# Attention over four images: inverse sums applied to the mixed banks, a sixth transferred group, half of the transferred tiles in heads and tails

## The chip, the core and the metric

The kernel runs on one core of one Trainium2 chip. A core has TensorE (matrix products, transposes), VectorE, ScalarE, Pool (GpSimd) and SyncE, each with a queue of instructions that it works off in order; they wait for one another on semaphores. TensorE writes PSUM; VectorE and ScalarE read it; Pool sees only SBUF. Transfers are issued by SyncE here and run on 16 DMA engines. The metric is the time of one execution in microseconds (us); shown are medians of several runs.

## The reference, cut to what matters

For each of four images x of 128 channels by 1024 positions:

```
y   = group_norm(x, 4 groups) * gamma + beta
q, k, v = (w_qkv y + b_qkv) split in three        # 128 channels each
w   = softmax(q^T k / sqrt(128))                  # 1024 x 1024
out = x + w_out (v w^T) + b_out
```

All in float32.

## The kernel before, in words

Weights are folded first: the scores become z^T y plus a bias per key, with z a projection of y, and v already contains w_out. Nothing is left behind the mix but a bias and the sum with x.

The queries of the four images make 32 blocks of 128, eight for an image; four blocks make a group (0 to 7). The loop has a turn for each block. Each engine's queue has its own copy of this loop, with the order written out by hand; what is said below of a turn holds for the engine named.

- TensorE (from L645): the scores of the block two turns ahead (`block_scores`, L700): three fp32r products, z and y each parted in a head (rounded to fp32r) and a tail (the rest), over two halves of 512 keys, 6 instructions. Then `turn` (L720), eight transposes, for blocks of groups 0, 6 and 7. Then pieces of the next image's projections (`projection`, L665): Z0 and Z1 in turns 4 and 7 of an image, the value jobs V0, V1, V2 in turns 5, 6 and the next image's 0. Then some tiles of an earlier group's mix (`mix`, L737), as the table `MIX` says; a group has 8 tiles of 128 keys by 512 queries. The mix of group g begins in turn 4g + 7.
- VectorE: `maximum` of the block two turns ahead (L513), with the key bias; for a turned block, half of the copy out of PSUM (L534); for a block of groups 1 to 5 `flip` (L547), a transposition of 32x32 squares into a staging buffer; pieces of the projections (`z_tail` L487, `projection_vectors`); `results` of a group (L556); `inverse_sum` of the block two turns ahead (L530); statistics of the image two ahead.
- ScalarE: copies out of PSUM, `exponentials` (L359) with the row sums, `y_head`.
- Pool: `normalise` (L293) multiplies each block's probabilities by its inverse sums; `normalised_input`, `y_tail`, and `z_tail` (L281) of the second half.
- SyncE: `swap` (L228) of a group: 16 transfers of 128 KB from staging to home, which put the flipped squares in their places; `store` of results.

What a block goes through: scores, maximum, exponential, inverse sum, normalisation on Pool, then either transposes on TensorE or flip and transfer, then the mix. Groups 1 to 5 are mixed as whole f32 tiles (`L765`), groups 6 and 7 as three fp32r products of heads and tails (`L760` to `L762`). `probs` has four buffers; a block's exponential waits until the block four before it has been turned or flipped.

An image's first scores wait for its z tail:

```
                if b > 0 and i == 0:
                    pe.wait_ge(s_z_lo, HALVES * (b - 1) + 1)
                    pe.wait_ge(s_y_lo, HALVES * b)
```

Of the kernel before, what the change touches and what calls it, by code (L numbers as in the profile page):

```python
# [5 lines left out]
def attention_kernel(nc, x, vectors, weights, out):  # L6
# [38 lines left out]
    SWAPPED = range(1, 6)  # L45
    SPLIT_GROUPS = (6, 7)
    HOME = (0, 1, 0, 1, 0, 1)
    SWAP = 16 * SQ * SQ
    MIX = {4: [(0, 1)], 5: [(0, 1)], 6: [(0, 1)], 7: [(0, 1)], 8: [(0, 1)], 9: [(0, 1)], 10: [(0, 2)],
           27: [(5, 2)], 28: [(5, 3)], 29: [(5, 2)], 30: [(5, 1), (6, 3)], 31: [(6, 5)]}  # L50
# [8 lines left out]
    with ctx:  # L59
# [19 lines left out]
        minus_mean = sb("minus_mean", [128, 128])  # L79
# [19 lines left out]

        y = sb("y", [C, 2, N])  # L100
        y_hi, y_lo = sb("y_hi", [C, 2, N], fp32r), sb("y_lo", [C, 2, N], fp32r)
        z_hi, z_lo = sb("z_hi", [C, 2, N], fp32r), sb("z_lo", [C, 2, N], fp32r)
        z_full = sb("z_full", [C, HALF])
        v = sb("v", [128, 2, KT, C])
        v_hi, v_lo = sb("v_hi", [128, KT, C], fp32r), sb("v_lo", [128, KT, C], fp32r)

        key_bias = sb("key_bias", [128, 2, BLOCKS])
        neg_max = sb("neg_max", [128, BLOCKS])
        first_max = sb("first_max", [128, 1])
        row_sum = sb("row_sum", [128, BLOCKS])  # L110
        inv_sum = sb("inv_sum", [128, BLOCKS])
        probs = sb("probs", [128, RING, N])

        with nc.sbuf_tensor("crossed", [128, 4, GROUP], fp32) as crossed:
            pass
        pt_hi_7 = sb("last_turned_head", [128, KT, HALF], fp32r)
        sb("home_of_group_5", [128, KT, HALF], fp32r)
        pt_hi_6 = sb("group_6_turned_head", [128, KT, HALF], fp32r)
        pt_lo_7 = sb("last_turned_tail", [128, KT, HALF], fp32r)
        pt_lo_6 = sb("group_6_turned_tail", [128, KT, HALF], fp32r)  # L120
        PT_HI, PT_LO = {6: pt_hi_6, 7: pt_hi_7}, {6: pt_lo_6, 7: pt_lo_7}
        result = sb("result", [C, 2, HALF])

# [4 lines left out]
        DEV, MINUS_MEAN, VARIANCE = 400, 408, 416  # L128
# [34 lines left out]
        s_v_lo = sem("last_v_tail_ready")  # L163
        s_y = sem("y_ready")
# [11 lines left out]
        s_inv = sem("inv_sum_ready")  # L176
# [5 lines left out]
        s_swapped = [sem("squares_swapped_even"), sem("squares_swapped_odd")]  # L182
        s_mixed = sem("mixed_tiles_done")
        s_result = sem("result_ready")
        s_stored = [sem("stored_even"), sem("stored_odd")]
# [21 lines left out]

        def copy_of_turned(home, n, j):

            return home[:, 4 * j:4 * j + 4, n % QB * 128:(n % QB + 1) * 128]  # L210

        def whole_home(group):
            return crossed[:, HOME[group], :].rearrange("p (v q) -> p v q", v=KT)

# [4 lines left out]
        def _(sp):  # L219
# [7 lines left out]

            def swap(group):  # L228
                sp.wait_ge(s_flipped, QB * group)
                if group > 1:  # L230
                    sp.wait_ge(s_mixed, KT * (group - 1))
                for k in range(SQ):
                    for g in (0, 2, 1, 3):
                        t = g ^ k
                        sp.dma_start(crossed[32 * t:32 * t + 32, group % 2, g * N:(g + 1) * N],  # L235
                                     crossed[32 * g:32 * g + 32, 2 + group % 2, t * N:(t + 1) * N]
                                     ).then_inc(s_swapped[group % 2], 16)
# [6 lines left out]
            swap(1)  # L244
            for group in range(2, 6):
                swap(group)
                store(group - 2)
            for group in range(4, GROUPS_OF_FOUR):
                store(group)
            for g in range(HALVES):  # L250
                sp.wait_ge(s_stored[g], 16 * BATCHES)

        @block_ctx.gpsimd
        def _(pool):
# [12 lines left out]
            pool.tensor_scalar(minus_mean[:, :], group_mean[:, :], -1.0, None, ALU.mult).then_inc(s_const, 1)  # L267
# [13 lines left out]
            def z_tail(b):  # L281
                pool.wait_ge(s_z_full, b)
                pool.tensor_tensor(z_lo[:, b % 2, HALF:N], z_full[:, :], z_hi[:, b % 2, HALF:N].bitcast(fp32),
                                   ALU.subtract).then_inc(s_z_lo, 1)

# [7 lines left out]
            def normalise(b, i):  # L293
                pool.wait_ge(s_inv, BLOCKS * b + i + 1)
                pool.tensor_scalar(probs[:, i % RING, :], probs[:, i % RING, :], inv_sum[:, i:i + 1], 1.0,  # L295
                                   ALU.mult, ALU.mult).then_inc(s_probs, 1)
# [12 lines left out]
            normalise(0, 0)  # L309
            rstd_of(1, 2, 2)  # L310
            normalise(0, 1)
            for b in range(BATCHES):
                for i in range(BLOCKS):
                    behind = 0 < b < BATCHES - 1 and i == 3
                    if behind:
                        y_tail(b + 1, 0)
                    if b == 0 and i in (2, 3):
                        y_tail(1, i - 2)
                    if after(b, i, 2)[0] < BATCHES:
                        normalise(*after(b, i, 2))  # L320
                    if behind:
                        y_tail(b + 1, 1)
                    if 0 < b < BATCHES - 1 and i == 0:
                        rstd_of(b + 1, b + 2, b + 2)
                    if i == (0 if b == 0 else 1) and b + 1 < BATCHES:
                        normalised_input(b + 1)
                    if i == 7 and b + 1 < BATCHES:
                        z_tail(b + 1)

        @block_ctx.scalar  # L330
        def _(act):
# [7 lines left out]
            def value_copy(b, job, bank):  # L339
                lo, hi = V_TILES[job]  # L340
                if b == 2:
                    act.wait_ge(s_mixed, KT * (HALVES * (b - 1) - 1) + hi)
                act.activation(v_hi[:, lo:hi, :] if b == BATCHES - 1 else v[:, b % 2, lo:hi, :],
# [3 lines left out]
            def projection_copy(b, job, bank):  # L347
# [4 lines left out]
                half = slice(0, HALF) if job == Z0 else slice(HALF, N)  # L352
                act.activation(z_hi[:, b % 2, half], bank, ACT.Identity, bias=z_bias[:, :]).then_inc(s_z_hi, 1)  # L353
                if job == Z1:
                    if b >= 2:
                        act.wait_ge(s_z_lo, HALVES * (b - 1))
                    act.activation(z_full[:, :], bank, ACT.Identity, bias=z_bias[:, :]).then_inc(s_z_full, 1)

            def exponentials(b, i):  # L359
                act.wait_ge(s_max, BLOCKS * b + i + 1)  # L360
                freed = BLOCKS * b + i - RING
# [4 lines left out]
                act.activation(probs[:, i % RING, :], scores[:, i % 2, :], ACT.Exp,  # L366
                               bias=neg_max[:, i:i + 1], scale=-1.0, accum_out=row_sum[:, i:i + 1]).then_inc(s_exp, 1)

            def turned_copy(n):
                group = n // QB  # L370
                if group == 6:
                    act.wait_ge(s_swapped[0], swaps(4))
                if group == 7:
                    act.wait_ge(s_mixed, KT * 5)
                act.wait_ge(s_turned, 2 * turns(n) + 1)
                if group not in SPLIT_GROUPS:
                    act.activation(copy_of_turned(whole_home(group), n, 0), turned_tiles(0), ACT.Copy).then_inc(s_copied[0], 1)
                    return
                for j in range(2):
# [506 lines left out]
```

## Time and profile before

| | |
|---|---|
| time, median of 3 runs | 146.07 us (144.9 to 148.31) |
| span of the profiled execution | 143.7 us; its own time beside the span is not listed, the median lies 2.4 us above it |
| TensorE busy | 133.6 us (93%), 589 matmuls |
| VectorE, ScalarE, Pool busy | 103.9, 67.7, 57.1 us |
| granted TensorE clock | 0.997 mean |
| transfers of groups 1 to 5 | 80 of 128 KB, 2.3 us to landing |
| chain that ended last | PE 66%, DVE 14%, SP's queue 7% |

In the profile PE is TensorE, PEld its weight loads, DVE VectorE, ACT ScalarE, POOL Pool, SPq the queue of SyncE. L12 is line 12 of the kernel. A tile's name stands left of the arrow where it is written. Successive matmuls overlap, so the time of one is longer than the distance to the next; prices are taken from start to start. The chain of waits is followed back from the last instruction, at each step to what released it.

### The profile page before, as it was taken

Reading aid. Unit: us, or ns where it says so; the run is one execution under the profiler, and the core shown is the slowest. Engines: PE = TensorE matmul, PEld = TensorE weight load, DVE = VectorE, ACT = ScalarE, POOL = GpSimd, SP = SyncE. Lnnn points to the kernel's source line nnn. Section 1 sums busy time; section 2 is a strip of 40 time slices with the busy share of each in tenths; the row PEclk is TensorE's granted clock in tenths of the full one; section 3 lists DMA queues with packets and bytes.
Section 4 is the critical chain, followed back from the end, with each engine's and each line's share of the span. In section 5 each row is a group of like instructions: output and inputs, shape, how many; then the busy total and the mean of one; then the engine's idle time right before and its main releaser. Section 6 shows DMA issues by size and latency. Waiting matters only on the chain.

```text
span 143.7 us, 1862 instructions
## 1 busy us (share of the span) xinstructions
PE 133.6 (93%) x589; PEld 94.4 (66%) x589; DVE 103.9 (72%) x201; ACT 67.7 (47%) x122; POOL 57.1 (40%) x66
## 2 busy tenths in 40 slices
PE   7999999997499979997999999999999999999990
PEld 7978579873367635665655556766776666768770
DVE  0597587799978999899496987898763787463402
ACT  3164858763266526543361364455843666353000
POOL 6032347963334666633355556433543213330000
PEclk9999999999999999999999999999999999999998
DMA  4940000000045976983598539973996001000211
GB/s 159 310 188 0 0 5 0 0 2 0 0 101 117 206 165 141 206 200 109 109 203 197 152 66 206 206 182 81 212 203 168 0 0 73 0 0 0 80 70 73
DMA packets 6154, 15.07 MB, mean 105 GB/s; under 512 B 1664, under 2 KB 1664, under 8 KB 6144
## 3 DMA queue, kind: packets, MB, share of 16 engines
q1 hardware_dynamic: 5856, 14.69, 41.3%
q10 hardware_dynamic: 288, 0.27, 0.5%
q8 instruction: 5, 0.08, 0.3%
q14 instruction: 5, 0.04, 0.1%
HBM read 2.36 MB, written 2.10 MB: 31 GB/s over the span
## 4 chain that ended last, share of the span: by engine, by line
PE 66%; DVE 14%; SPq 7%; issue 5%; ACT 4%; DMA 2%; DVEq 0%
PE mixed L765 22%; SPq L235 7%; PE scores L715 5%; PE scores L714 5%; PE turned L731 5%; PE scores L717 5%; DVE scores L527 5%; PE scores L773 4%; DVE crossed L552 4%; ACT probs L366 3%; PE mixed L760 3%; PE mixed L762 3%; PE mixed L761 3%; PE turned L661 2%; PE mixed L661 2%
## 5 line engine op out<-in xcount | busy, mean ns | idle before, releaser
L295 POOL TENSOR_SCALAR probs<-probs,inv_sum 128x1024 f32<-128x1024 f32 x32 | 35.9, 1122 | 63.7 <-DVE inv_sum L532 63.7
L527 DVE TENSOR_SCALAR_CACHE_REDUCE scores<-scores,key_bias 128x1024 f32<-128x1024 f32 x31 | 40.0, 1289 | 13.9 <-PE scores L717 13.8
L366 ACT ACTIVATE probs<-scores,neg_max 128x1024 f32<-128x1024 f32 x32 | 35.7, 1115 | 18.7 <-DVE scores L527 17.7
L765 PE MATMUL mixed<-crossed,v 128*128 128x512 f32 x80 | 37.7, 593 | 1.0 <-DMA crossed<-crossed 1.0
L714 PE MATMUL scores<-y_hi,z_hi 128*128 128x512 f32 x62 | 34.6, 558 | 0.3 <-DVE z_lo L489 0.3
L552 DVE STREAM_TRANSPOSE crossed<-probs 128x1024 f32<-128x1024 f32 x20 | 24.8, 1241 | 0.0
L715 PE MATMUL scores<-y_lo,z_hi 128*128 128x512 f32 x62 | 24.4, 394 | 0.0
L765 PEld LDWEIGHTS mixed<-crossed,v 128*128 128x128 f32 x80 | 14.1, 190 | 11.6 <-issue 11.0
L717 PE MATMUL scores<-y_hi,z_lo 128*128 128x512 f32 x62 | 19.3, 392 | 0.0
L714 PEld LDWEIGHTS scores<-y_hi,z_hi 128*128 128x128 f32 x62 | 11.7, 189 | 8.8 <-issue 5.7
L715 PEld LDWEIGHTS scores<-y_lo,z_hi 128*128 128x128 f32 x62 | 11.7, 189 | 7.0 <-issue 5.5
L717 PEld LDWEIGHTS scores<-y_hi,z_lo 128*128 128x128 f32 x62 | 11.6, 188 | 2.8
L731 PEld LDWEIGHTS turned<-ident,probs 128*128 128x128 f32 x96 | 11.1, 141 | 2.4 <-issue 1.0
L731 PE MATMUL turned<-ident,probs 128*128 128x128 f32 x96 | 12.5, 273 | 0.1
L532 DVE RECIPROCAL inv_sum<-row_sum 128x1 f32<-128x1 f32 x32 | 5.0, 157 | 7.4 <-ACT probs L366 6.6
L561 DVE SCALAR_TENSOR_TENSOR result<-mixed,out_bias,xs 128x512 f32<-128x512 f32 x8 | 5.9, 733 | 6.1 <-PE mixed L762 6.1
L353 ACT ACTIVATE z_hi<-turned,z_bias 128x512 fp32r<-128x512 f32 x6 | 4.1, 686 | 9.1 <-PE turned L695 9.1
L767 PE MATMUL mixed<-crossed,v 128*128 128x512 f32 x16 | 8.0, 592 | 0.0
L381 ACT ACTIVATE last_turned_head<-turned 128x512 fp32r<-128x512 f32 x8 | 4.3, 595 | 7.6 <-PE turned L731 7.6
L278 POOL TENSOR_TENSOR y_lo<-y,y_hi 128x512 fp32r<-128x512 f32 x6 | 7.7, 1280 | 0.0
L544 DVE TENSOR_TENSOR last_turned_tail<-turned,last_turned_head 128x512 fp32r<-128x512 f32 x8 | 5.1, 684 | 3.5 <-ACT last_turned_head L381 3.5
L381 ACT ACTIVATE group_turned_head<-turned 128x512 fp32r<-128x512 f32 x8 | 4.3, 594 | 6.9 <-PE turned L731 6.9
(147 smaller groups left out, 168.9 us busy)
## 6 DMA issues: line engine op xcount, KB each, us to landing
crossed<-crossed SPq DMA_DIRECT2D x80, 128.0 KB, 2.3
out_dram<-result SPq DMA_DIRECT2D x8, 256.0 KB, 2.5
xs<-in_x_dram SPq DMA_DIRECT2D x2, 512.0 KB, 6.4
xs<-in_x_dram SPq DMA_DIRECT2D x3, 256.0 KB, 5.0
xs<-in_x_dram ACTq DMA_DIRECT2D x1, 256.0 KB, 3.5
ws<-in_weights_dram SPq DMA_DIRECT2D x1, 256.0 KB, 3.7
vecs<-in_vectors_dram ACTq DMA_DIRECT2D x1, 3.0 KB, 3.9
```

The source lines that it names most:

```text
L235: sp.dma_start(crossed[32 * t:32 * t + 32, group % 2, g * N:(g + 1) * N], crossed[32 * g:32 * g + 32, 2 + group % 2, t * N:(t + 1) * N]).t ...
L295: pool.tensor_scalar(probs[:, i % RING, :], probs[:, i % RING, :], inv_sum[:, i:i + 1], 1.0, ALU.mult, ALU.mult).then_inc(s_probs, 1)
L366: act.activation(probs[:, i % RING, :], scores[:, i % 2, :], ACT.Exp, bias=neg_max[:, i:i + 1], scale=-1.0, accum_out=row_sum[:, i:i + 1]) ...
L381: act.activation(copy_of_turned(PT_HI[group], n, j), turned_tiles(j), ACT.Copy).then_inc(s_turned_hi, 1)
L527: dve.tensor_scalar(scores[:, i % 2, :], scores[:, i % 2, :], key_bias[:, b % 2, i:i + 1], None, ALU.subtract, ALU.min, accum_out=neg_max[ ...
L552: dve.transpose(crossed[:, 2 + group % 2, :].rearrange("p (tv u c) -> p tv u c", u=QB, c=32)[:, :, u, :], probs[:, n % RING, :].rearrange( ...
L714: pe.matmul(to[h], z_hi[:, b % 2, query], y_hi[:, b % 2, halves[h]], start=True, stop=False)
L715: pe.matmul(to[h], z_hi[:, b % 2, query], y_lo[:, b % 2, halves[h]], start=False, stop=False)
L717: mm = pe.matmul(to[h], z_lo[:, b % 2, query], y_hi[:, b % 2, halves[h]], start=False, stop=True)
L731: mm = pe.transpose(turned[:, j, k * 128:(k + 1) * 128], probs[:, n % RING, key:key + 128], ident[:, :])
L765: mm = pe.matmul(bank, v[:, b % 2, k, :], at, start=first, stop=final)
L767: mm = pe.matmul(bank, v[:, b % 2, k, :], whole_home(group)[:, k, :], start=first, stop=final)
```

## The change

- The probabilities of groups 0 to 6 are no longer normalised block by block. Pool's `normalise` and VectorE's `inverse_sum` stay for the last group (blocks 28 to 31) alone. For the other groups VectorE makes one reciprocal of four columns (`group_inverse_sums`); SyncE stores it into a scratch in DRAM, element by element (`inv_out`), in front of the group's `swap`, and behind it loads it back, spread over all 128 partitions (`inv_in`). VectorE multiplies the mixed bank by it (`scaled`, in the place of `results`), and Pool adds x (`residual`). `out_bias` is added to x by ScalarE (`add_out_bias`).
- `flip` and the turns of group 0 wait for the exponential.
- Group 6 is flipped and transferred too, not turned. Its mix stands at the end, between two halves of 256 queries of group 7 (`mix_last`).
- Of groups 1 to 5 the tiles 4 to 7 (pairs 2 and 3), of group 6 all, are parted in heads (ScalarE, `swapped_heads`, 128x1024 for a pair of tiles) and tails (Pool, `tails`; for group 6 VectorE, `last_tails`), and mixed as three fp32r products. The values are parted for this by Pool (`part_values`).
- The first z tail of an image goes from VectorE to Pool, reading a copy that ScalarE makes; the channel statistics move from turns 4 and 5 to 2 and 3; the mean is negated on VectorE instead of by a second matmul.

The core of the diff:

```diff
-    SWAPPED = range(1, 6)
-    SPLIT_GROUPS = (6, 7)
+    SWAPPED = range(1, 7)
+    LAST = GROUPS_OF_FOUR - 1
+    PARTED = {group: (2, 3) for group in range(1, 6)} | {6: (0, 1, 2, 3)}
+    WHOLE = 4
     MIX = {4: [(0, 1)], 5: [(0, 1)], 6: [(0, 1)], 7: [(0, 1)], 8: [(0, 1)], 9: [(0, 1)], 10: [(0, 2)],
-           27: [(5, 2)], 28: [(5, 3)], 29: [(5, 2)], 30: [(5, 1), (6, 3)], 31: [(6, 5)]}
+           27: [(5, 2)], 28: [(5, 2)], 29: [(5, 2)], 30: [(5, 2)]}
...
+            def inv_out(group):
+                sp.wait_ge(s_inv, group + 1)
+                sp.dma_start(inv_scratch[group, :].rearrange("(u p) -> p u", u=QB),
+                             inv_sum[:, QB * group:QB * group + QB],
+                             allow_slow_non_contiguous=True).then_inc(s_scratch, 16)
+
+            def inv_in(group):
+                sp.wait_ge(s_scratch, 16 * (group + 1))
+                if group >= 2:
+                    sp.wait_ge(s_scaled, group - 1)
+                sp.dma_start(inv_rows[:, group % 2, :],
+                             inv_scratch[group:group + 1, :].to_broadcast([128, HALF])).then_inc(s_inv_rows[group % 2], 16)
...
+            inv_out(0)
+            inv_in(0)
+            for group in SWAPPED:
+                inv_out(group)
                 swap(group)
+                inv_in(group)
+                if group >= 2:
+                    store(group - 2)
...
+            def z_tail(b, h):
+                half = slice(h * HALF, (h + 1) * HALF)
+                pool.wait_ge(s_z_full, HALVES * (b - 1) + h + 1)
+                pool.tensor_tensor(z_lo[:, b % 2, half], z_full[:, h, :], z_hi[:, b % 2, half].bitcast(fp32),
                                    ALU.subtract).then_inc(s_z_lo, 1)
...
+            def tails(group, pair):
+                pool.wait_ge(s_head, parts(group, pair))
+                pool.tensor_tensor(home_pair(group, pair), home_pair(group, pair).bitcast(fp32),
+                                   head_pair(group, pair).bitcast(fp32), ALU.subtract).then_inc(s_tail, 1)
...
+                    if QB * LAST <= n + 2 < BATCHES * BLOCKS:
+                        normalise(n + 2)
...
+                    if i == 0 and b > 0:
+                        tails(2 * b - 2, 3) if b > 1 else None
+                        residual(2 * b - 3) if b > 1 else None
+                    if i == (1 if b == 0 else 2) and not last:
                         y_tail(b + 1, 0)
...
+                    if i == 2 and not last:
+                        part_values(b)
+                    if i == 3 and b > 0:
+                        tails(2 * b - 1, 2)
+                    if i == 4 and b > 0:
+                        if not last:
+                            y_tail(b + 1, 1)
+                        tails(2 * b - 1, 3)
+                        residual(2 * b - 2)
+                    if i == 4 and not last:
+                        z_tail(b + 1, 0)
+                    if i == 7 and not last:
+                        z_tail(b + 1, 1)
+                    if i == 7 and 0 < b and not last:
+                        tails(2 * b, 2)
+            residual(5)
+            residual(6)
...
+            # ScalarE, in a turn, behind exponentials and y_head
+                    if 11 <= n < 28 and i in (3, 7):
+                        swapped_heads(n // QB - 1, 2)
+                    if n >= 12 and i in (4, 0) and n <= 28:
+                        swapped_heads(n // QB - 2, 3)
...
+            # ScalarE, at the head of a turn
+                    if n >= 30:
+                        swapped_heads(6, 2 * (n - 30))
+                    if not swapped(n):
+                        turned_copy(n)
+                    if n >= 30:
+                        swapped_heads(6, 2 * (n - 30) + 1)
...
+            # VectorE, behind the loop
+            last_tails(0)
+            turned_tails(30)
+            scaled(5)
+            last_tails(1)
+            turned_tails(31)
+            last_tails(2)
+            last_tails(3)
+            last_result(0, mixed[:, 1, 0:256])
+            scaled(6)
+            last_result(1, scores[:, 0, 0:256])
...
+            # TensorE, behind the loop
-            mix(GROUPS_OF_FOUR - 1, KT)
+            mix_last(0, mixed[:, 1, 0:256])
+            mix(6, KT)
+            mix_last(1, scores[:, 0, 0:256])
```

## Rows read from the trace of the kernel before

**Rows 1.** Windows: stretch, length, busy of PE, PEld, DVE, ACT, POOL; clock, DMA share, GB/s.
```profile
29.27:40.24 10.97, 8.10 (x37) 5.39 (x37) 10.86 (x21) 4.98 (x10) 4.10 (x4) 1.00 0.00 0
40.24:53.85 13.61, 12.57 (x49) 8.43 (x49) 11.86 (x23) 6.85 (x12) 7.44 (x7) 1.00 0.71 156
53.85:63.20 9.35, 9.35 (x34) 5.84 (x34) 8.45 (x16) 4.79 (x9) 5.83 (x5) 1.00 0.82 180
63.20:87.14 23.94, 22.61 (x83) 14.04 (x82) 19.78 (x39) 11.13 (x19) 10.91 (x10) 1.00 0.61 144
87.14:93.85 6.71, 6.71 (x29) 4.63 (x28) 5.26 (x11) 2.54 (x7) 3.47 (x3) 1.00 0.95 211
93.85:109.82 15.97, 15.97 (x70) 10.88 (x70) 12.55 (x26) 9.88 (x18) 6.15 (x6) 1.00 0.75 175
109.82:140.46 30.64, 30.60 (x140) 21.92 (x139) 15.18 (x28) 10.89 (x20) 5.20 (x5) 1.00 0.09 31
```

**Rows 2.** Chain that ended last: start, us on the chain, what, instructions.
```profile
40.24 0.58 SPq L235
...
51.42 2.29 DMA crossed<-crossed
53.85 2.81 PE mixed L765 x6
...
77.50 2.58 PE mixed L765 x6
...
81.00 0.46 PE scores L717 x2
...
95.23 0.67 PE turned L661 x6
...
106.37 0.87 PE turned L731 x8
```

**Rows 3.** Groups by form: busy us, mean ns of one, idle before, releaser.
```profile
L527 DVE TENSOR_SCALAR_CACHE_REDUCE scores<-scores,key_bias 128x1024 f32<-128x1024 f32 x31 | 40.0, 1289 | 13.9 <-PE scores L717 13.8
L366 ACT ACTIVATE probs<-scores,neg_max 128x1024 f32<-128x1024 f32 x32 | 35.7, 1115 | 18.7 <-DVE scores L527 17.7 <-DVE neg_max L522 0.7
L552 DVE STREAM_TRANSPOSE crossed<-probs 128x1024 f32<-128x1024 f32 x20 | 24.8, 1241 | 0.0
L278 POOL TENSOR_TENSOR y_lo<-y,y_hi 128x512 fp32r<-128x512 f32 x6 | 7.7, 1280 | 0.0
L544 DVE TENSOR_TENSOR last_turned_tail<-turned,last_turned_head 128x512 fp32r<-128x512 f32 x8 | 5.1, 684 | 3.5 <-ACT last_turned_head L381 3.5
L532 DVE RECIPROCAL inv_sum<-row_sum 128x1 f32<-128x1 f32 x32 | 5.0, 157 | 7.4 <-ACT probs L366 6.6
L353 ACT ACTIVATE z_hi<-turned,z_bias 128x512 fp32r<-128x512 f32 x6 | 4.1, 686 | 9.1 <-PE turned L695 9.1
L290 POOL TENSOR_SCALAR y<-xs,norm_a,norm_b 128x1024 f32<-128x1024 f32 x3 | 3.6, 1192 | 0.2
L337 ACT ACTIVATE y_hi<-y 128x1024 fp32r<-128x1024 f32 x3 | 3.2, 1052 | 0.0
L489 DVE SCALAR_TENSOR_TENSOR z_lo<-turned,z_bias,z_hi 128x512 fp32r<-128x512 f32 x3 | 2.1, 708 | 0.0
L307 POOL TENSOR_TENSOR y_lo<-y,y_hi 128x384 fp32r<-128x384 f32 x1 | 1.0, 1017 | 1.7 <-ACT y_hi L399 1.7
```

**Rows 4.** Timeline of SyncE's queue, the fifth transfer's sixteen issues: start, us, what.
```profile
98.10 10.03 SPq L235 DMA_DIRECT2D crossed<-crossed  x16
```

**Rows 5.** DMA queues (packets, MB, share of 16 engines' span) and issues (KB, us to landing).
```profile
q1 hardware_dynamic: 5856, 14.69, 41.3%
q10 hardware_dynamic: 288, 0.27, 0.5%
...
crossed<-crossed SPq DMA_DIRECT2D x80, 128.0 KB, 2.3
```

**Rows 6.** Waits of TensorE: us in total, times, longest us.
```profile
PE turned L648 <- DVE mean_var L452: 3.6, 2, 2.6
```

More of the change, by code:

```diff
@@ L112, in attention_kernel @@
+        inv_sum = sb("inv_sum", [128, BATCHES * BLOCKS])
         probs = sb("probs", [128, RING, N])
[L114 to L120 removed]
@@ L206, in swaps, with parts, head_slot, home_pair @@
             return SWAP * len([g for g in SWAPPED if g <= group and g % 2 == group % 2])
+        def parts(group, pair):
+            return sum(len(PARTED[g]) for g in range(1, group)) + PARTED[group].index(pair) + 1
+        def head_slot(group, pair):
+            return pair if group == 6 else 2 * (group % 2) + pair - 2
+        def home_pair(group, pair):
+            return HOME[group % 2][:, :].rearrange("p (g w) -> p g w", g=SQ)[:, :, 256 * pair:256 * pair + 256]
+        def head_pair(group, pair):
+            return heads[:, head_slot(group, pair), :].rearrange("p (g w) -> p g w", g=SQ)
+        def tile_of(home, k, tiles):
+            return home.rearrange("p (g v u c) -> p v u g c", g=SQ, v=tiles, u=QB)[:, k, :, :, :]
         def copy_of_turned(home, n, j):
             return home[:, 4 * j:4 * j + 4, n % QB * 128:(n % QB + 1) * 128]
-        def whole_home(group):
-            return crossed[:, HOME[group], :].rearrange("p (v q) -> p v q", v=KT)
         def turned_tiles(j):
@@ L375, in turned_copy @@
[L375 to L379, printed above, removed]
-                    act.wait_ge(s_turned, 2 * turns(n) + j + 1)
-                    act.activation(copy_of_turned(PT_HI[group], n, j), turned_tiles(j),
-                                   ACT.Copy).then_inc(s_turned_hi, 1)
+                if n // QB == LAST:
+                    act.wait_ge(s_swapped[1], swaps(5))
+                    for j in range(2):
+                        act.wait_ge(s_turned, 2 * turns(n) + j + 1)
+                        act.activation(copy_of_turned(pt_hi, n, j), turned_tiles(j), ACT.Copy).then_inc(s_turned_hi, 1)
+                    return
@@ L735, in _, with three_products @@
             tiles_mixed = [0] * GROUPS_OF_FOUR
+            def three_products(bank, value, head, tail, first, final):
+                value_hi, value_lo = value
+                pe.matmul(bank, value_hi, head, start=first, stop=False)
+                pe.matmul(bank, value_hi, tail, start=False, stop=False)
+                return pe.matmul(bank, value_lo, head, start=False, stop=final)
             def mix(group, count):
@@ L750, in mix @@
                         pe.wait_ge(s_v, 3 * (b + 1))
[L751 removed]
+                        if b == BATCHES - 1:
                             pe.wait_ge(s_v_lo, 3)
[L753 to L757 removed]
```

375 lines of the change are left out of this document (224 added, 151 removed).

## Prediction, before any run of the changed kernel

> **What bounds the kernel now.** Blocks are numbered 0 to 31 through the four images; turn n of the loop issues the scores of block n+2. I cut the span at the events that the change touches and read the busy times by stage [rows 1]. From 29.27 to 40.24 us VectorE is the bound: 10.86 of 10.97 us busy, TensorE 8.10. From 40.24 to 53.85 the first transfer is: the chain of waits [rows 2] goes through its sixteen issues to the landing at 51.42 + 2.29, and TensorE starts the first transferred tile at 53.85. From there on TensorE is busy for 9.35 of 9.35, 22.61 of 23.94, 6.71 of 6.71, 15.97 of 15.97 and 30.60 of 30.64. So up to 53.85 a gain must come from VectorE or the transfer, after that from TensorE, as long as nothing new stops TensorE. The granted clock is 1.00 (2.4 GHz) in all these stages.
>
> **TensorE's prices** [rows 2], start to start: a whole f32 tile is two instructions, 2 x 2.58/6 = 0.86; an fp32r product is 0.46/2 = 0.23, so a parted tile is 0.70; eight transposes 0.87; scores 6 x 0.23 = 1.40; three value tiles 0.67. The change parts 20 tiles of groups 1 to 5, 20 x 0.16 = 3.3 us, and drops the transposes of group 6, 4 x 0.87 = 3.5 us: all on the path this would be minus 6.8. No row shows an fp32r product over the 32-element chunks that a parted tile streams; its price lies between 0.23 and the 0.43 of an f32 instruction. I take 0.23, since whole tiles stream such chunks already.
>
> **Up to the first tile (minus 1.7).** VectorE loses a reciprocal per block with its wait for the exponential (32 x 157 ns, 7.4 us of idle before them) and the z tail of 708 ns [rows 3]; the flip waits for the exponential, no longer for Pool. It gains a negated mean (0.2) and a reciprocal per group; two statistics move two turns ahead, into turns 2 and 3. I walk its queue with 1.20 from a maximum to the next operation, 1.15 for a flip, 0.6 for a copy or a half's statistics, 0.2 for a key bias, and TensorE's scores where they are later: the maxima of blocks 2 to 8 start at 18.05, 20.85, 23.55, 26.1, 29.9, 32.25 and 34.8, the flip of block 7 runs from 36.0 to 37.15. With the group's reciprocal SyncE could start at 37.3, 2.9 ahead of 40.24 [rows 2]. But in front of the sixteen transfers now stands the store of the inverse sums, 512 single elements. Its issue I take at 0.6, as a transfer's (10.03/16) [rows 4]; its packets lie between nothing and 32 per DMA engine at 162 ns, the mean of queue q1 (41.3% of 16 x 143.7 over 5856), 5.2 us; short ones are nearest to q10's mean, 40 ns (0.5%, 288), so 1.3 [rows 5], half of it hidden under the issues: 0.6. The Trainium skill (DMA: Bandwidth & Descriptors, Rules for kernel authors) says that a non-contiguous last dimension lowers to one descriptor per element, which speaks against this store; no row shows such a transfer. First tile: 53.85 - 2.9 + 1.2 = 52.15. TensorE is there at about 48.5 (turns 4 to 10 by the prices, 20.6, and scores, from 26.5) and waits some 3.5.
>
> **The new wait (plus 4.0 and plus 3.8).** The first z tail of the next image leaves VectorE for Pool, into turn 4 of an image, and stands there behind the last pair's tail of the transferred group and behind a residual. That pair's tail waits for its head, which ScalarE makes behind this turn's exponential. TensorE's scores of the next image's first block, two turns later, wait for the z tail, and all later scores, mixes and projections stand behind them. From the start of block 14's scores: scores ready at 1.6, maximum to 2.95; the projection is ready at 2.3, ScalarE copies it twice (z_full is new for this half; 2 x 0.6) to 3.5; exponential to 4.6; head, 128x1024 as y_hi's 1052 ns, to 5.5; Pool's subtraction of 128x1024 to 7.9; residual to 9.2; z tail to 10.45 [rows 3]. That subtraction is in no row: two-input ones take 1017 ns at 384 columns and 1280 at 512, a line that gives 2.33; the ends are 1.19 (one input, 1024) and 2 x 1.28 = 2.56. TensorE's own work in the two turns is 1.4 + 0.7 + 0.86 + 0.70 and 1.4 + 0.67 + 0.70 = 6.4, so it stands still for 4.1. Block 14's scores start 2.8 behind the first tile, so this stage takes 2.8 + 10.55 = 13.35 and not 9.35. At block 24 (turns 20 to 22) the same makes 10.5 of 6.71; there the pair before it, behind the parted values in Pool's queue, holds TensorE for 1 us inside the same span. In the first image Pool has no tails, and its z tail is early (31.5, wanted at 32.6).
>
> **Between and behind these (minus 2.85, minus 2.0).** Turns 14 to 19: scores 8.4, values and means 0.87, projection 0.7, the last value job 0.9 with its wait for the scaled group, seven whole tiles 6.0, six parted 4.2: 21.1 against 23.94. Parted tiles give 1.0 of it; the idle 1.3 of the stage goes, since the channel means that end one such wait [rows 6] are ready three turns earlier; the rest is a pair of mean matmuls and waits inside busy rows. The third transfer lands 1.4 ahead of its tile. Turns 22 to 25: 3.5 + 3.0 + 3.9 + 3.6 = 14.0 against 15.97, two turns' transposes and 0.16 for each of four parted tiles less. VectorE has some 3.1 us a turn (maximum, flip, a share of the rest) under TensorE's 3.5; Pool 21 an image and ScalarE as much, under 28. So the 28 normalisations that Pool drops (1.12 each) are worth nothing themselves here.
>
> **The end (plus 2.4, minus 0.3).** Before: 30.64 from block 28's scores to the last result [rows 1]. After, from the same event: flip of block 27 and the reciprocal to 4.15; store of the sums 1.2; transfer 6 lands 11.75 after its start, as the fifth (last issue 0.6 before the end of 10.03, then 2.3) [rows 4, 5]: at 17.1. TensorE has done turns 26 to 30 at 15.85 and cannot go on: ScalarE's copy of block 30 stands behind the first head of group 6, VectorE's tails of block 30 behind that pair's tail, and the transposition of block 31 waits for them. Head 1.15, pair's tail 1.2 (twice the form of 684 ns, less a start), half of block 30's tails 0.65 [rows 3]: the transposition starts at 17.1 + 3.05, after 4.3 of standing still. Group 5 is scaled at 4.25, the first half of group 7 takes 24 x 0.12 = 2.9, group 6 24 x 0.23 = 5.6, the second half 2.9, the last drain 0.25: 17.1 + 15.95 = 33.05. (0.12 for 256 columns lies between 0.112, a value pass of 129 columns, and 0.23.) VectorE's other pair tails, done at 9.0, keep ahead of group 6. The last sum has 256 columns, not 512: minus 0.3.
>
> **The sum:** - 1.7 + 4.0 - 2.85 + 3.8 - 2.0 + 2.4 - 0.3 = + 3.35. The span was 143.7; the median of the three runs shown is 146.07, 2.4 above it (what lies around the span, and the spread; the lowest is 144.9). The forecast is 146.07 + 3.35 = **149.4 us**, 2.3% more. Two per cent (2.9 us) is about what a measurement of this kernel can tell from no change, so it stands near the edge.
>
> **Rivals.**
> 1. *Pool fits under TensorE* (not slower). Place: the z tails of blocks 16 and 24. If Pool's two-input operations cost what one-input ones do (1.19, and 0.65 at 512), the chain is 8.0 and each stall 1.6: 2 x 2.45 less, 144.5. If the chain is ready at 6.4, where it stops to matter, 8.1 go: 141.3. For it: Pool's spans are rough by the page's own word, and ScalarE may make the head while it waits for the maximum. Against: even with free tails the other links make 8.0. Chance 0.36.
> 2. *The clock falls in the new gaps* (slower). TensorE stands still for 3.5, 4.1, 3.8 and 4.3 us; the longest wait of before is 2.6 [rows 6], at 1.00. If the next turn's work (3.7, 3.5, 2.9) runs at 1.2 GHz it takes twice as long: 3 for one gap, 10 for three; I take 4, 153.5. The Trainium skill (TensorE: Matmul & The Clock Gate, The HAM clock gate) says that an idle tensor engine is throttled to 1.2 GHz; no row of before shows it. Chance 0.14.
> 3. *The single-element stores are slow.* At 5.2 of packets in front of a transfer, not 0.6, the first tile and the last transfer come 4.6 later each: 158.6. Chance 0.06.
> 4. *The parting saves nothing*: at 0.43 a product, a parted tile costs 1.29, 20 x 0.59 more: 161. Chance 0.04.
>
> **The numbers.** Forecast 0.40, its own range 147 to 152, a little over half of it above 2%. Slower: 0.23 of it and rivals 2 to 4, 0.47. Same: 0.17, and 0.12 of rival 1 (144.5): 0.29. Faster: 0.24, the rest of rival 1. The range 142 to 154 leaves out the bottom of rival 1 and the top of rivals 2 to 4, about 0.2.
>
> **What would show it.** TensorE idle for about 4 us ahead of the scores of blocks 16 and 24, ended by Pool's z tail, which follows a 128x1024 subtraction and a residual without a gap; the first tile near 52; TensorE idle some 4 us ahead of the last transposition, group 6's transfer landing just before; the clock at 1.00 in these stages; a pitch of 0.23 in the parted tiles. It is wrong if Pool's 128x1024 subtraction is near 1.2, if something else ends those waits, or if the clock or the small store shows.

## The result, and the profile after

The changed kernel takes **160.56 us** (median of four runs, 159.66 to 162.04) against 146.01 of the kernel before on the same chip: ratio 1.103, 95% interval 1.095 to 1.112. It is slower, as forecast, but by 14.5 us and not by 3.4. The profiled execution has a span of 158.5 us, 14.8 more than before. From here on, ratios are to the kernel before, run beside each kernel on its chip; 0.01 is 1.46 us. The ratios and the gains in us worked out from them leave out executions that stand clearly above the fastest of their kernel; the medians do not.

The head of the page of the changed kernel: busy tenths of TensorE and its granted clock in forty slices of 4 us.

```profile
span 158.5 us, 1917 instructions
...
PE   7999999999991799279999899199998799249992
...
PEclk9999999999999579959999999879999999955999
```

TensorE stands still in four places, and behind each the clock row falls; before, the clock was 1.00 in every stage [rows 1]. The stages from the first group's transfer on, cut at the same events as [rows 1] (first transferred tile, scores of blocks 16, 22, 24 and 28, last result); columns as there.

```profile
40.24:52.65 12.41, 8.04 (x31) 5.01 (x30) 9.61 (x18) 6.27 (x11) 5.01 (x6) 0.92 0.92 166
52.65:68.26 15.61, 11.66 (x35) 6.96 (x35) 7.58 (x11) 6.98 (x10) 8.43 (x6) 0.83 0.76 161
68.26:92.02 23.76, 22.98 (x86) 16.07 (x87) 16.78 (x29) 12.60 (x20) 11.20 (x9) 0.94 0.69 132
92.02:102.40 10.38, 6.63 (x31) 4.58 (x29) 5.47 (x8) 6.39 (x10) 9.31 (x6) 0.98 0.81 142
102.40:118.17 15.77, 15.50 (x58) 11.18 (x59) 11.04 (x18) 8.23 (x13) 6.29 (x4) 0.91 0.75 127
118.17:155.76 37.59, 31.07 (x155) 24.92 (x153) 19.08 (x31) 16.23 (x25) 14.81 (x10) 0.91 0.50 115
```

Set against the forecast's own stages (lengths in us; the third row is the kernel with fillers of the experiments, in which the gaps are there but the clock stays up; a record that overlaps the one before it counts from that one's end):

| | first tile at | to block 16 | to 22 | to 24 | to 28 | to last result |
|---|---|---|---|---|---|---|
| forecast | 52.15 | 13.35 | 21.1 | 10.5 | 14.0 | 33.05 |
| changed kernel | 52.65 | 15.61 | 23.76 | 10.38 | 15.77 | 37.59 |
| with fillers | 51.92 | 13.28 | 21.8 | 10.7 | 14.1 | 35.4 |

The miss is 0.50 + 2.26 + 2.66 - 0.12 + 1.77 + 4.54 = 11.6 us. **The waits were foreseen; what they set off stood only among the rivals.** TensorE's timeline in the changed kernel, the instructions in front of which it stood still longest, and the third group's first tile: start, us, line, what, and in brackets the idle time and what ended it.

```profile
52.65 5.26 PE L921 MATMUL mixed<-home_odd,v 128*128 128x512 f32 x6 [4.38 <-DMA home_odd<-staging_odd]
68.26 0.80 PE L854 MATMUL scores<-y_hi,z_hi 128*128 128x512 f32 x1 [3.95 <-POOL z_lo L341]
...
89.21 2.81 PE L921 MATMUL mixed<-home_odd,v 128*128 128x512 f32 x6 [0.51 <-DMA home_odd<-staging_odd]
...
102.40 0.79 PE L854 MATMUL scores<-y_hi,z_hi 128*128 128x512 f32 x1 [3.31 <-POOL z_lo L341]
...
140.91 1.94 PE L874 MATMUL turned<-ident,probs 128*128 128x128 f32 x8 [5.16 <-DVE last_turned_tail L663]
```

Forecast were 3.5, 4.1, 3.8 and 4.3 us for the four long ones, and no wait for the third group. The second in detail, from the timeline (ScalarE and Pool, other rows left out):

```profile
60.60 0.68 ACT L448 ACTIVATE z_full<-turned,z_bias 128x512 f32<-128x512 f32 x1
...
62.26 1.06 ACT L479 ACTIVATE heads<-home_odd 128x1024 fp32r<-128x1024 f32 x1
63.40 2.36 POOL L354 TENSOR_TENSOR home_odd<-home_odd,heads 128x1024 fp32r<-128x1024 f32 x1 [6.16 <-ACT heads L479]
...
65.72 1.27 POOL L361 TENSOR_TENSOR result<-result,xs 128x512 f32<-128x512 f32 x1
66.94 1.26 POOL L341 TENSOR_TENSOR z_lo<-z_full,z_hi 128x512 fp32r<-128x512 f32 x1
```

The z tail's input is there at 61.28; Pool had been idle for 6.16 us and takes it up only at 66.94, behind the subtraction of 128x1024 (2.36, forecast 2.33) and the residual. Now windows over the gaps and the work behind them, same columns, the clock third from the right:

```profile
48.27:52.65 4.38, 0.01 (x2) 0.03 (x1) 1.93 (x5) 2.40 (x6) 3.07 (x3) 0.78 0.91 230
52.65:57.91 5.26, 5.26 (x7) 2.32 (x8) 2.58 (x4) 0.94 (x1) 3.62 (x3) 0.53 1.09 159
68.26:71.20 2.94, 2.94 (x8) 2.37 (x8) 0.00 (x0) 0.00 (x0) 0.00 (x0) 0.50 0.11 39
102.40:105.30 2.90, 2.90 (x7) 2.32 (x8) 0.00 (x0) 0.00 (x0) 0.00 (x0) 0.50 0.81 213
135.75:140.91 5.16, 0.00 (x1) 0.03 (x1) 1.97 (x3) 3.06 (x5) 0.08 (x1) 0.86 0.66 164
140.91:146.50 5.59, 5.59 (x27) 5.59 (x28) 5.59 (x7) 3.01 (x4) 2.13 (x1) 0.52 0.13 47
```

In each of these four gaps the clock falls, and the work behind the gap runs at 0.50 to 0.53, the 1.2 GHz level: three whole tiles take 5.26 and not 2.81 [rows 2], six score products 2.9 and not 1.40, eight transposes 1.94 and not 0.87 [rows 2].

And the small store. DMA queue and issues of the changed kernel (KB, us from issue to landing), and the sixth group's issues in SyncE's queue with its last landing (from the chain that ended last):

```profile
q1 hardware_dynamic: 11472, 18.63, 55.9%
...
home_odd<-staging_odd SPq DMA_DIRECT2D x48, 128.0 KB, 5.9
home_even<-staging_even SPq DMA_DIRECT2D x48, 128.0 KB, 3.7
...
inv_scratch<-inv_sum SPq DMA_DIRECT2D x7, 2.0 KB, 8.9
```
```profile
122.21 0.37 SPq L266 DMA_DIRECT2D inv_scratch<-inv_sum  x1
122.67 13.39 SPq L284 DMA_DIRECT2D home_even<-staging_even  x16
...
135.47 2.35 DMA home_even<-staging_even
```

Two KB take 8.9 us to land. The transfers behind them land in 5.9 and 3.7 us where they took 2.3 [rows 5], and sixteen issues took 10.03 [rows 4], now 13.39 (12.57 for the first group, 13.48 for the fourth, 10.0 for the others). From the store's issue to the first head made of what landed (137.85) are 15.64 us; the forecast allowed 1.2 + 11.75.

### The profile page after: what moved, and what is told of

It is laid out like the page before. It is cut to its first block, busy times and chain, and to the rows that moved or that the text cites. A ratio compares the mean times of both kernels' runs of the same rounds, so it can differ in the third digit from the quotient of the medians.

```text
span 158.5 us, 1917 instructions
## 1 busy us (share of the span) xinstructions
PE 134.8 (85%) x593; PEld 100.3 (63%) x593; DVE 101.9 (64%) x180; ACT 83.0 (52%) x135; POOL 68.0 (43%) x63
## 4 chain that ended last, share of the span: by engine, by line
PE 54%; POOL 14%; issue 12%; SPq 8%; DVE 7%; ACT 2%; DMA 1%; DVEq 0%; POOLq 0%
SPq L284 8%; PE scores L854 7%; PE scores L857 6%; PE scores L855 6%; POOL home_odd L354 6%; PE scores L943 4%; PE turned L874 3%; PE mixed L882 3%; PE mixed L883 3%; PE mixed L884 3%; PE mixed L921 3%; POOL y_lo L335 3%; DVE staging_even L676 3%; PE mixed L906 3%; PE turned L801 2%
## 5 line engine op out<-in xcount | busy, mean ns | idle before, releaser
L921 PE MATMUL mixed<-home_odd,v 128*128 128x512 f32 x24 | 14.0, 713 | 6.2 <-DMA home_odd<-staging_odd 6.2
L341 POOL TENSOR_TENSOR z_lo<-z_full,z_hi 128x512 fp32r<-128x512 f32 x6 | 7.7, 1279 | 26.3 <-ACT z_full L448 26.3
L354 POOL TENSOR_TENSOR home_odd<-home_odd,heads 128x1024 fp32r<-128x1024 f32 x6 | 14.2, 2366 | 8.1 <-ACT heads L479 8.1
L361 POOL TENSOR_TENSOR result<-result,xs 128x512 f32<-128x512 f32 x7 | 9.8, 1406 | 15.8 <-DVE result L686 15.8
L676 DVE STREAM_TRANSPOSE staging_odd<-probs 128x1024 f32<-128x1024 f32 x12 | 14.9, 1239 | 2.5 <-DMA home_odd<-staging_odd 2.5
L676 DVE STREAM_TRANSPOSE staging_even<-probs 128x1024 f32<-128x1024 f32 x12 | 14.9, 1239 | 0.0
L921 PEld LDWEIGHTS mixed<-home_odd,v 128*128 128x128 f32 x24 | 5.0, 224 | 11.6 <-issue 11.4
L335 POOL TENSOR_TENSOR y_lo<-y,y_hi 128x512 fp32r<-128x512 f32 x6 | 7.6, 1282 | 10.5 <-ACT y_hi L430 10.5
L354 POOL TENSOR_TENSOR home_even<-home_even,heads 128x1024 fp32r<-128x1024 f32 x4 | 9.5, 2380 | 1.7 <-ACT heads L479 1.7
L882 PE MATMUL mixed<-heads,v_hi 128*128 128x512 f32 x20 | 9.7, 487 | 0.4 <-POOL home_odd L354 0.4
L479 ACT ACTIVATE heads<-home_even 128x1024 fp32r<-128x1024 f32 x8 | 8.3, 1056 | 3.1 <-DMA home_even<-staging_even 3.1
```

The costliest lines, as they stand in the source:

```text
L335: pool.tensor_tensor(y_lo[:, b % 2, half], y[:, b % 2, half], y_hi[:, b % 2, half].bitcast(fp32), ALU.subtract).then_inc(s_y_lo, 1)
L354: pool.tensor_tensor(home_pair(group, pair), home_pair(group, pair).bitcast(fp32), head_pair(group, pair).bitcast(fp32), ALU.subtract).the ...
L676: dve.transpose(STAGING[group % 2][:, :].rearrange("p (tv u c) -> p tv u c", u=QB, c=32)[:, :, u, :], probs[:, n % RING, :].rearrange("p ( ...
L882: pe.matmul(bank, value_hi, head, start=first, stop=False)
L921: mm = pe.matmul(bank, v[:, b, k, :], tile_of(HOME[g][:, :].bitcast(fp32), k, KT), start=first, stop=final)
```

## The experiments

Theory A says that three costs add up: Pool's queue ahead of two z tails, the single-element store beside each transfer, and the clock behind each gap. All kernels start from the changed one.

**1. The z tail first in Pool's queue.**

```
 if i == 4 and b > 0:
     if not last:
         y_tail(b + 1, 1)
+        z_tail(b + 1, 0)
     tails(2 * b - 1, 3)
     residual(2 * b - 2)
-if i == 4 and not last:
-    z_tail(b + 1, 0)
+if i == 4 and b == 0:
+    z_tail(1, 0)
```

> From the changed kernel (160.6 us), with one move in Pool's queue: in turn 4 of images 1 and 2 the first z tail of the next image stands ahead of the last pair's tail and the residual, not behind them. Theory A (three costs add up: Pool's queue ahead of the z tails, the store of the inverse sums in front of each transfer, the clock that falls in TensorE's gaps): the waits of 3.95 and 3.31 us ahead of the scores of blocks 16 and 24 shrink to under 1, those scores stream at 0.23 and not 0.43 (another 1.3 and 1.4), the store and the end stay: 160.6 - 10 = 150 to 152. Rival B (the z tail is only the last of several links that are equally late, ScalarE's copies or the transfer of the group): the waits stay above 2.5 us with another cause, 157 to 160.

Measured: median 149.37, ratio 1.017 (1.002 to 1.032), by the ratios 12.6 us less. Waits of TensorE (us in total, times, longest):

```profile
PE mixed L922 <- DMA home_odd<-staging_odd: 6.8, 2, 5.6
PE turned L875 <- DVE last_turned_tail L664: 4.9, 1, 4.9
...
PE mixed L883 <- POOL home_odd L354: 1.0, 1, 1.0
```

The waits for Pool's z tail are gone from the list; those for the transfers stay. Rival B falls. What the move costs is a wait of 1.0 for Pool's tails.

**2. The transfers ahead of the store.**

```
-inv_out(group)
 swap(group)
+inv_out(group)
 inv_in(group)
```

> From the changed kernel, with one exchange in SyncE's queue: each group's sixteen transfers are issued ahead of the store of its inverse sums, not behind it. Theory A: the sixteen issues take 10.0 us for every group (now 12.6, 13.5 and 13.4 for groups 1, 4 and 6), the first transferred tile starts near 49.7 (now 52.65), the wait ahead of it is short enough for the clock to stay up, the last transfer lands some 3 us earlier against the end of block 31: together 6 to 10 us, 150 to 154. Rival C (the store is hidden beside the issues, and the transfers are late because VectorE and the 232 GB/s of the queue make them so): the issues stay at 12 to 13, less than 1.5 us in all, 159 to 160.6.

Measured: 174.46, ratio 1.201 (1.186 to 1.216): slower than the changed kernel by another 14 us, which neither theory expected. SyncE's queue shows why:

```profile
56.76 10.04 SPq L284 DMA_DIRECT2D home_even<-staging_even  x16
66.84 0.58 SPq L266 DMA_DIRECT2D inv_scratch<-inv_sum  x1
74.93 0.33 SPq L274 DMA_DIRECT2D inv_rows<-inv_scratch  x1
...
75.83 10.05 SPq L284 DMA_DIRECT2D home_odd<-staging_odd  x16
```

The issues do take 10.0 again, but the load that reads the sums back waits for the store to land and comes 8.1 us after it, time in which SyncE issues nothing else; before this exchange the store landed under the sixteen issues. One group now costs SyncE 19.1 us (56.76 to 75.83) and TensorE waits 14.4 us for transfers. My expectation counted the issues and left out the wait in the same queue. It tells nothing for or against C.

**3. Fillers in the gaps.** Products that nobody reads, ahead of the wait that makes each gap:

```
+def fill(bank, count):
+    for _ in range(count):
+        pe.matmul(bank, fold_hi[:, :], y_hi[:, 1, 0:HALF], start=True, stop=True)
...
+if k == 0 and group == 1:
+    fill(bank, 16)
 if k == 0:
     pe.wait_ge(s_swapped[g], swaps(group))
```

and the same with 16 and 13 ahead of the wait for the z tail, in the bank of the scores to come, and with 18 ahead of block 31's transposition, in the bank of its scores, already read.

> From the changed kernel, with TensorE kept at work where it now stands still: 16 products of 512 columns whose results nobody reads ahead of the first transferred tile, 16 ahead of block 16's scores, 13 ahead of block 24's, 18 ahead of block 31's transposition (0.23 us each at full clock, so 3.7, 3.7, 3.0 and 4.1 us inside the waits of 4.4, 3.95, 3.3 and 5.0). No wait is taken away. Theory A: the granted clock stays at 1.00 behind each of the four places, three whole tiles take 2.8 and not 5.3, the scores of blocks 16 and 24 1.4 and not 2.9, the transposition 0.9 and not 1.9, the first half's 24 products 2.9 and not 5.6: 7 to 8 us less, 152 to 154. Rival D (the slow pitch is not the clock's doing but that of the transfers and copies that run beside it, or the work would wait for the next transfer anyway): the pitches stay, or the gain is under 2 us, 158.5 to 161.

Measured: ratio 1.046 (1.032 to 1.060). Its four executions took 151.13, 152.76, 155.51 and 281.48 us; the profiled one is that of 281.48, which I do not compare, so the kernel ran again:

> The kernel with fillers in the four gaps once more, for the rows of its trace (runs of it so far: 151.1 and 152.8 us). Theory A: no wait is gone, but behind each gap the granted clock reads 1.00: three whole tiles in 2.8, the scores of blocks 16 and 24 in 1.4 each, the transposition in 0.9, 24 products of 256 columns in 2.9; 151 to 153. Rival D: the pitches behind the gaps stay at twice these.

Measured: 150.77, ratio 1.035 (1.026 to 1.045), 9.9 us less than the changed kernel. Windows over the work behind the four gaps, in the same order as above (the last one holds transposition, copies and the 24 products of 256 columns):

```profile
51.92:54.76 2.84, 2.84 (x7) 1.40 (x8) 2.62 (x4) 1.04 (x1) 2.34 (x2) 1.00 1.11 183
65.20:66.60 1.40, 1.40 (x6) 1.18 (x7) 0.00 (x0) 0.00 (x0) 0.00 (x0) 1.00 0.21 76
97.55:98.95 1.40, 1.40 (x8) 1.14 (x8) 0.00 (x0) 0.00 (x0) 0.00 (x0) 1.00 0.56 190
134.23:138.50 4.27, 4.17 (x33) 3.79 (x33) 4.27 (x6) 2.87 (x5) 2.14 (x1) 1.00 0.01 4
```

No wait was taken away, yet the clock reads 1.00 and every pitch is back: rival D falls. The same transfers and copies run beside the first tiles (DMA share 1.11 against 1.09). The Trainium skill (TensorE: Matmul & The Clock Gate, What's actually happening) says that an idle tensor engine is clocked at half rate; these rows agree.

**4. The store in pieces of 16 bytes.**

```
-inv_scratch[group, :].rearrange("(u p) -> p u", u=QB)
+inv_scratch[group, :].rearrange("(p u) -> p u", u=QB)
```

> From the changed kernel, with the store of the inverse sums in 128 pieces of 16 bytes, not 512 of 4 bytes; the sums so land in another order, and the queries of a group are scaled by one another's sums. Everything else, the order in SyncE's queue too, is as it was. Theory A, with the price per element: the store lands in about a quarter of its 7.9 to 9.5 us beyond a start of some 2, 3.5 to 4.5, and most of what the store costs comes back: 152 to 156. Rival E (the price is that of a store in front, whatever its pieces): it still lands in 7 to 9 us, 159 to 161.

Measured: 152.96, ratio 1.054 (1.044 to 1.064), 7.2 us less, with SyncE's order untouched. Queue and issues, and the sixth group's:

```profile
q1 hardware_dynamic: 8784, 18.63, 50.3%
...
home_odd<-staging_odd SPq DMA_DIRECT2D x48, 128.0 KB, 2.3
home_even<-staging_even SPq DMA_DIRECT2D x48, 128.0 KB, 2.4
...
inv_scratch<-inv_sum SPq DMA_DIRECT2D x7, 2.0 KB, 1.9
```
```profile
119.18 0.32 SPq L266 DMA_DIRECT2D inv_scratch<-inv_sum  x1
119.60 10.05 SPq L284 DMA_DIRECT2D home_even<-staging_even  x16
```

The same 2 KB land in 1.9 us, lower than expected, and all transfers in 2.3 again. From store to first head: 131.47 - 119.18 = 12.29, 3.35 less than with single elements. Rivals E and C fall. Queue q1 has 2688 packets fewer, 7 x (512 - 128): one for each piece. The Trainium skill (DMA: Bandwidth & Descriptors, Rules for kernel authors) says that a non-contiguous last dimension lowers to one descriptor per element; the count agrees.

**5. No parting in groups 1 to 5.** `PARTED` empty for them; heads, tails and parted values of these groups go.

> From the changed kernel, with one part of the change undone: no tile of groups 1 to 5 is parted, so ScalarE makes no heads and Pool no tails and no parted values for them; group 6 stays as it is. Theory A (the tail of the last pair and the residual in Pool's queue hold the z tails of blocks 16 and 24): 20 tiles cost TensorE 0.16 us more each, 3.3 in all, but the two waits of 3.95 and 3.31 go, and the slow scores behind them: 160.6 + 3.3 - 7.3 - 2.7 = 154, and so the parting, meant to spare TensorE work, costs more than it spares. Rival F (the waits are the residual's or ScalarE's doing, with or without tails): they stay, 163 to 164.

Measured: 150.73, ratio 1.036 (1.031 to 1.040), 9.9 us less. TensorE's waits:

```profile
PE turned L862 <- DVE last_turned_tail L651: 6.7, 1, 6.7
PE mixed L909 <- DMA home_odd<-staging_odd: 3.3, 1, 3.3
```

No wait for a z tail: without the tail ahead of it, residual and all, it is early. Rival F falls, and the gain is larger than I expected, so the 3.3 us that parting should spare TensorE are not all there (experiment 11).

**6. Both repairs.** Experiments 1 and 4 together, with the scaling reading the sums in their new order:

```
-dve.tensor_tensor(result[:, g, :], mixed[:, g, :], inv_rows[:, g, :], ALU.mult)
+dve.tensor_tensor(result[:, g, :].rearrange("p (u q) -> p u q", u=QB),
+                  mixed[:, g, :].rearrange("p (u q) -> p u q", u=QB),
+                  inv_rows[:, g, :].rearrange("p (q u) -> p u q", u=QB), ALU.mult)
```

> From the changed kernel, two repairs together: the z tail ahead of the tail and the residual in Pool's queue, and the sums stored in 128 pieces of 16 bytes, with the scaling reading them back in that order (every fourth element), so that each query gets its own sum. Theory A, with the costs as separate terms: 160.6 - 11.2 (z tails first alone, 149.4) - 7.6 (wide store alone, 153.0) = 142, with the scaling at its old duration; 141 to 144, below the kernel before. Rival G (the two gains overlap: where TensorE no longer waits for Pool it waits for the transfers, and the other way round): 145 to 148.

Measured: 143.58, ratio 0.988 (0.982 to 0.994), inside A's range; G falls. That is 16.9 us less than the changed kernel, where the two alone give 12.6 + 7.2 = 19.8. The difference of 2.9 us is no larger than what the intervals of the four ratios leave open (some 3.0 together), so an overlap is not shown. Against the kernel before it is 1.2% less, clear of 1 but inside the 2% that I count as no change. The scaling reads every fourth element at 1.07 us instead of 0.67.

**7. Both repairs and fillers** ahead of the first tile and block 31's transposition, 12 each:

> The two repairs as in the run with both, and 12 products that nobody reads ahead of the first transferred tile and 12 ahead of block 31's transposition. Theory A: the granted clock stays at 1.00 behind both gaps; of the 2.3 and 2.8 us that it cost there, 3 to 5 us come back against the run with both repairs: 137 to 140. Rival D (what follows waits for the next transfer or for VectorE anyway): less than 1.5 us.

Measured: 141.82, ratio 0.976 (0.970 to 0.982), 1.8 us less than experiment 6: short of theory A, a little above rival D. The clock is 1.00 throughout, but in the trace of experiment 6 it had not fallen ahead of the first tile either:

```profile
50.08 2.81 PE L924 MATMUL mixed<-home_odd,v 128*128 128x512 f32 x6 [2.25 <-DMA home_odd<-staging_odd]
```

There only the end was left to win. In the other three executions of experiment 6 the mean clock was 0.976, in the profiled one 0.988; where it fell in those, no trace shows.

**8. The end in another order.** ScalarE and VectorE finish blocks 30 and 31 ahead of group 6's pairs:

```
-if n >= 30: swapped_heads(6, 2 * (n - 30))        # ahead of turned_copy(n)
-if n >= 30: swapped_heads(6, 2 * (n - 30) + 1)    # behind it
+for pair in range(PAIRS): swapped_heads(6, pair)  # behind the last turn
-last_tails(0); turned_tails(30); scaled(5); last_tails(1); turned_tails(31); last_tails(2); last_tails(3)
+turned_tails(30); scaled(5); turned_tails(31); last_tails(0) ... last_tails(3)
```

> From the changed kernel, with one exchange at the end: ScalarE copies the heads of blocks 30 and 31, and VectorE makes their tails, ahead of the four pairs of group 6, so that block 31's transposition and the first half of group 7 no longer wait for the sixth transfer. Theory A: TensorE does those while the transfer lands (137.8 us in the changed kernel) and starts group 6 some 2.5 us behind the landing, at 140.5 and not 146.5; the last result comes 5 to 6.5 us earlier, 154 to 156. Rival H (VectorE's pair tails, four of 1.2 us now in a row, hold group 6 itself, and the clock falls there instead): less than 3 us, 157.5 to 160.

Measured: ratio 1.037 (1.028 to 1.046), by the ratios 9.7 us less. In its trace (the execution of 156.3 us) the transposition starts 0.51 us after TensorE came free, and group 6 waits 1.23 for the first pair's tail:

```profile
137.07 1.09 PE L870 MATMUL turned<-ident,probs 128*128 128x128 f32 x8 [0.51 <-POOL probs L373]
...
142.47 0.47 PE L878 MATMUL mixed<-heads,last_v_hi 128*128 128x512 f32 x1 [1.23 <-DVE home_even L666]
```

From block 28's scores to the last result are 30.8 us, not 37.59: 6.8 less, near the 5 to 6.5 expected. The other 2.9 of the 9.7 this edit does not explain; its executions spread from 150.52 to 156.3. Rival H falls: the pair tails keep up.

**9. All repairs together**, with 12 fillers ahead of the first tile only:

> All repairs together: z tail first in Pool's queue, the sums stored in 128 pieces and read back in that order, 12 products that nobody reads ahead of the first transferred tile, and the end in the order of the run before this one, without fillers there. Against the 141.8 us of the kernel with fillers at both places: theory A, the sixth transfer (landing near 121) is covered by the transposition and the first half, 3 to 4.5 us less, 137.5 to 139; rival H, the pair tails hold group 6: 140 to 142.

Measured: **138.79 us, ratio 0.952** (0.946 to 0.958), the lowest median of all and within theory A. The row of TensorE's clock:

```profile
PEclk9999999999999999999999999999999999999999
```

**10. The single elements through ScalarE's queue**, with one semaphore for each group; SyncE keeps the load behind the transfers.

> From the changed kernel, with the store of the inverse sums, 512 elements of 4 bytes as before, issued by ScalarE on its own queue in the third turn of a group, and no longer by SyncE in front of the sixteen transfers; SyncE reads the sums back behind them as before. Theory J (what the elements delay is what stands behind them in the same queue): the transfers land as with the wide store, 152 to 154. Rival K (the elements occupy the DMA engines themselves, so any transfer at the same time is delayed, whichever queue they come from): 158 to 161.

Measured: 159.16, ratio 1.094 (1.085 to 1.103). Issues:

```profile
home_odd<-staging_odd SPq DMA_DIRECT2D x48, 128.0 KB, 5.0
...
inv_scratch<-inv_sum ACTq DMA_DIRECT2D x7, 2.0 KB, 8.3
```

Theory J falls, K holds. The elements take as long on another queue and hold up transfers that they do not stand in front of: the sixth group's, first issued at 120.41, gave its first head at 137.10, 16.7 us later (119.60 to 131.47, 11.9, with 16-byte pieces). The Trainium skill (DMA: Bandwidth & Descriptors, Issuing engines are not separate DMA queues) says that all issuers share the same sixteen DMA engines; the rows agree.

**11. All repairs, no parting in groups 1 to 5.**

> The kernel with all repairs (138.8 us), with the tiles of groups 1 to 5 whole. Theory A: with Pool's queue no longer in the way, the parting is worth what TensorE's prices say, 20 x 0.16 = 3.3 us, so 141 to 142.5 without it. Rival L (the parted tiles' own waits for Pool's tails and the work they give ScalarE and Pool eat most of it): 138.5 to 140.2.

Measured: 139.50, ratio 0.960 (0.955 to 0.965) against 0.952 (0.946 to 0.958): the parting is worth some 1.1 us, and as the intervals overlap it is not shown to be worth anything. The time lies in rival L's range. The kernel with parting waits 1.2 us for a Pool tail in front of group 3's parted tiles, and from block 22's to block 24's scores it takes 8.23 where TensorE is busy for 7.03. Where the rest of the 3.3 goes is not shown.

## Why the prediction was wrong

**The path up to the first tile: nearly right.** The store was issued at 37.05 (forecast 37.3); the first tile came 0.5 late. The fixed part, the walk of VectorE's queue, held.

**The new wait: right.** Place, cause and size were as written: 3.95 and 3.31 us of standing still (forecast 4.1 and 3.8), ended by Pool's z tail behind a 128x1024 subtraction of 2.36 (forecast 2.33) and a residual. Experiments 1 and 5 take it away from either side. Rival 1 is out, its price of 1.19 for the subtraction too. Rival 4 is out: parted products run at a pitch of 0.23 to 0.24.

**The clock: the step that failed.** The forecast had no term for it and asked for "the clock at 1.00 in these stages". It foresaw gaps of 3.5 to 4.3 us, saw that the longest in the trace was 2.6 [rows 6], at 1.00, and so stood outside what the rows covered; it gave the fall, as rival 2, a chance of 0.14 and 4 us, between bounds of 3 and 10. The gaps came, and the clock fell in all four: 5.26 - 2.81 = 2.45 behind the first, 2.94 - 1.40 and 2.90 - 1.40 = 3.04 behind the next two, and at the end 14.85 us from the transposition to the last result instead of 12.9, 1.95: together 7.4 of the 11.6 us. Fillers alone, which leave every wait in place, bring the stages back to the forecast's within 0.7 us up to block 28 (table above), and the whole to 150.77 against the 149.4 forecast.

**The store: mis-sized.** "Short ones are nearest to q10's mean, 40 ns" gave 1.2 us. Rows of a trace without one single-element store carried the choice; the far end of the bound, 5.2 us of packets, was nearer. With 16-byte pieces the sixth transfer's first head comes 12.29 us after the store, with single elements 15.64, so the elements cost 3.35 more there. The forecast fell short by 0.5 us at the first tile and by 2.55 at the last landing (135.47 + 2.35 = 137.82; less 118.17 that is 19.65 behind block 28's scores, forecast 17.1). The third transfer, forecast to land 1.4 ahead of its tile, held that tile up by 0.51; with 16-byte pieces it does not. Alone, the wide store gives 7.2 us; in its trace the first tile comes 1.9 earlier, the three tiles behind that gap take 4.51 and not 5.26, and the end is 3.1 shorter. So a shorter gap also spares clock: rivals 2 and 3 are not separate cases but feed one another, and I had given them chances as if one excluded the other.

**The end: right in form.** From landing to transposition 3.09 us (forecast 3.05). What made it 4.5 late was the transfer, 2.55, and the clock, 1.95. Experiment 8 shows that TensorE's wait for this landing comes from the order in which two engines took up its pairs: in another order, with the same store, it is gone.

So of the difference of 11.6 us, 7.4 are the clock, 3.6 the store (0.5 + 2.55 + 0.51), and 0.6 stays without a name, about what is left between blocks 16 and 22 (0.7 with fillers too).

## What to carry to other kernels

When a forecast contains a gap in TensorE longer than any in the trace at hand, price the work behind it at the lower clock and let that be part of the forecast, not a rival; a gap as short as one that left the clock up is no safe ground either (last section). When operations move to another engine, read that engine's queue at the moment of need: here the order of three lines was worth 12.6 us and the parting itself some 1, within the noise. The store of single elements was priced by its elements, from SyncE's queue and from ScalarE's alike, and taking it out of one queue position put its landing into another wait (experiment 2).

## What the hardware showed that was not expected

- 512 elements of 4 bytes take 8.0 to 8.9 us to land (medians of the kernels here), 128 pieces of 16 bytes 1.9 to 2.2: four times fewer pieces, about four times less. From another queue the elements delay the transfers as much (8.3 us; 5.0 for a transfer's landing that takes 2.3).
- The granted clock fell in gaps of 3.3 to 5.2 us (the changed kernel), 2.8 and 3.3 (experiments 4 and 5, three tiles in 4.51 and 5.46) and 2.54 (experiment 4, ahead of block 24's scores), and had not fallen behind gaps of 2.25 (experiment 6) and 2.62 (the 2.6 of [rows 6]; 1.00 in that stage of [rows 1]). So in these traces the length of a gap alone does not tell whether it falls: 2.54 did it, 2.62 did not. Experiment 4, the gap and the window behind it:

```profile
99.11 0.52 PE L854 MATMUL scores<-y_hi,z_hi 128*128 128x512 f32 x1 [2.54 <-POOL z_lo L341]
```
```profile
99.11:102.00 2.89, 2.89 (x9) 2.37 (x10) 0.10 (x1) 0.00 (x0) 0.00 (x0) 0.56 0.37 123
```

- The sixteen issues of a group can stall (3.95 us in one issue of the sixth group). With the same store in front the kernel of experiment 5 issues them in 10.04, and yet their first head comes 16.3 us after the store (111.80 to 128.14): the transfers land late with or without the stall. What the stall is remains open.
